# A fused tile kept in PSUM over four rotating banks, with every tail on VectorE

## The reference

```python
def ffn(x):                                   # x: (2, 512, 256)
    gate = silu((x @ q(gate_w)) * gate_scale) # (.., 768)
    up = (x @ q(up_w)) * up_scale
    return ((gate * up) @ q(down_w)) * down_scale

x = x + attention(layernorm(x))
x = x + ffn(layernorm(x))
x = x + s4d(layernorm(x))
x = x + ffn(layernorm(x))
```

## Time and profile before

| | before |
|---|---|
| median of three runs | 141.35 us (141.25 to 142.14) |
| span of the profiled execution | 140.5 us |
| mean granted clock of TensorE | 0.942 |
| TensorE matmul busy | 118.3 us (84%), 650 instructions |
| VectorE busy | 105.1 us (75%), 244 |
| GpSimd busy | 100.1 us (71%), 156 |
| ScalarE busy | 62.3 us (44%), 117 |
| tails on GpSimd (line 408) | 12, 14.6 us |
| tails on VectorE (line 850) | 12, 9.7 us |
| fuses on VectorE (line 843) | 24, 17.5 us |
| heads on ScalarE (line 560) | 24, 15.0 us |

### The profile page before, as it was taken

How to read it: one execution, slowest core, us unless ns; L and a number is a source line. 1 busy time by engine, 2 the same in 40 slices (tenths; PEclk the granted TensorE clock), 3 DMA queues, 4 the chain that set the end, 5 groups by cost and what they waited for, 6 DMA issues and landing times.

```text
span 140.5 us, 2050 instructions
## 1 busy us (share of the span) xinstructions
PE 118.3 (84%) x650; PEld 78.2 (56%) x650; DVE 105.1 (75%) x244; ACT 62.3 (44%) x117; POOL 100.1 (71%) x156
## 2 busy tenths in 40 slices
PE   5489999999999700899999999794999896999950
PEld 5466587585877400785456844453745465446640
DVE  0459999998885896059735699999999998656272
ACT  3124156532331103644795437394454474374500
POOL 6282899998899998997864175669879883029621
PEclk9968999999999995559999999999999999999996
DMA  3999700000000020000000000000000000001304
GB/s 129 281 320 361 225 3 7 2 0 0 0 1 0 0 71 4 7 0 0 0 0 0 0 0 0 2 0 0 0 0 0 0 0 5 0 0 40 109 0 149
DMA packets 5599, 6.03 MB, mean 43 GB/s; under 512 B 900, under 2 KB 4952, under 8 KB 5592
## 3 DMA queue, kind: packets, MB, share of 16 engines
q1 hardware_dynamic: 5464, 5.91, 12.8%
q0 software_dynamic: 128, 0.03, 0.1%
HBM read 4.89 MB, written 1.05 MB: 42 GB/s over the span
## 4 chain that ended last, share of the span: by engine, by line
PE 29%; DVE 29%; POOL 25%; issue 6%; ACT 4%; DMA 3%; SPq 1%; POOLq 0%; DVEq 0%; ACTq 0%
PE psum L1064 15%; PE psum L1077 7%; POOL s4d L304 5%; DVE stats L594 4%; PE psum L1002 3%; DMA x_in<-in_x 3%; DVE fused L843 3%; DVE scaled_down L791 3%; POOL rstd L280 3%; DVE h_rows L832 3%; PE psum L1025 2%; POOL gate L390 2%; POOL up L390 2%; POOL gate_raw L386 2%; POOL up_raw L386 2%
## 5 line engine op out<-in xcount | busy, mean ns | idle before, releaser
L408 POOL TENSOR_TENSOR f_tail<-fused,f_head 128x512 f16<-128x512 f32 x12 | 14.6, 1219 | 15.2 <-ACT f_head L560 15.2
L549 ACT ACTIVATE gated<-psum,scales 128x512 f32<-128x512 f32 x24 | 16.3, 681 | 15.0 <-PE psum L1064 15.0
L1077 PE MATMUL psum<-down,f_head 128*128 128x256 bf16 x96 | 22.0, 273 | 0.1
L1077 PE MATMUL psum<-down,f_tail 128*128 128x256 bf16 x96 | 22.0, 273 | 0.0
L843 DVE SCALAR_TENSOR_TENSOR fused<-psum,up_scales_fit,gated 128x512 f32<-128x512 f32 x24 | 17.5, 738 | 4.7 <-PE psum L1064 3.0
L560 ACT ACTIVATE f_head<-fused 128x512 f16<-128x512 f32 x24 | 15.0, 626 | 10.7 <-DVE fused L843 10.5
L1064 PE MATMUL psum<-h_head,up 128*128 128x512 f16 x48 | 14.3, 379 | 1.3 <-DVE fused L843 1.3
L850 DVE TENSOR_TENSOR f_tail<-fused,f_head 128x512 f16<-128x512 f32 x12 | 9.7, 809 | 7.1 <-ACT f_head L560 7.1
L1064 PE MATMUL psum<-h_tail,up 128*128 128x512 f16 x48 | 14.3, 379 | 0.0
L1064 PE MATMUL psum<-h_head,gate 128*128 128x512 f16 x48 | 14.3, 379 | 0.0
L1064 PE MATMUL psum<-h_tail,gate 128*128 128x512 f16 x48 | 14.3, 379 | 0.0
(11 more groups left out here) (168 smaller groups left out, 267.9 us busy)
## 6 DMA issues: line engine op xcount, KB each, us to landing
x_in<-in_x SPq DMA_DIRECT2D x4, 256.0 KB, 4.4
out<-x_in SPq DMA_DIRECT2D x4, 256.0 KB, 2.1
qkv_sb<-in_qkv SPq DMA_DIRECT2D x3, 256.0 KB, 3.9
gate_raw<-in_gate_w SPq DMA_DIRECT2D x1, 768.0 KB, 6.8
up_raw<-in_up_w SPq DMA_DIRECT2D x1, 768.0 KB, 8.6
down_raw<-in_down_w SPq DMA_DIRECT2D x1, 768.0 KB, 10.3
wo_sb<-in_o_proj SPq DMA_DIRECT2D x1, 256.0 KB, 5.1
taps_all<-taps_dram SPq DMA_DIRECT2D x1, 256.0 KB, 3.0
```

Source lines behind the costliest of these rows:

```text
L408: pool.tensor_tensor(f_tail[:, m, :], fused[:, m % FUSED, :], f_head[:, m, :], ALU.subtract).then_inc(f_tail_by_pool, 1)
L549: act.activation(gated[:, m % 2, :], psum[:, BANK_GATE[m % 2], :], ACT.Silu, scale=gate_scales[:, m:m + 1]).then_inc(gated_ready, 1)
L1077: last = pe.matmul(column(BANK_DOWN[t // 2], H * (t % 2), H), part[:, m, t * P:t * P + P], down16[:, m, :], start=(m == 0 and t % 2 == 0 a ...
```

## The change

- `fused` is no longer a tile in SBUF: `fuse` writes in place over up's PSUM bank, and head and tail read it there.
- Up has the banks 7, 3, 4, 5, 7, 3 for the tiles 0 to 5, so four banks go round; 4 and 5 are those of the transposed rows, which are free once `h_tail` is made.
- GpSimd makes no tails (all three of its tails in each pass are gone from its program). VectorE makes all six of a pass, one tile behind its fuse where the order is regular; in passes 1 and 2 the hand-written order is as in the diff, with fuse 5 moved behind `norm_rows`.
- TensorE's up matmuls wait for the tail that frees their bank, no longer for the fuse two tiles back. `turn_h` waits for the first four tails of the pass and no longer for `h_tail`.
- The loop over passes in TensorE's program is written out four times.

```diff
-        FUSED = 4
-        fused = sb("fused", [P, FUSED, S])
...
-        POOL_TAILS = (1, 3, 4)
-        DVE_TAILS = tuple(m for m in range(M) if m not in POOL_TAILS)
...
-        BANK_H, BANK_GATE, BANK_UP, BANK_DOWN = [4, 5], [6, 2], [7, 3], [0, 1]
+        BANK_H, BANK_GATE, BANK_UP, BANK_DOWN = [4, 5], [6, 2], [7, 3, 4, 5, 7, 3], [0, 1]
...
-                    act.activation(f_head[:, m, :], fused[:, m % FUSED, :], ACT.Copy).then_inc(f_head_ready, 1)
+                    act.activation(f_head[:, m, :], psum[:, BANK_UP[m], :], ACT.Copy).then_inc(f_head_ready, 1)
...
-                if i >= FUSED and (m - FUSED) % M in POOL_TAILS:
-
-                    dve.wait_ge(f_tail_by_pool, len(POOL_TAILS) * ((i - FUSED) // M) + POOL_TAILS.index((m - FUSED) % M) + 1)
-                dve.scalar_tensor_tensor(out=fused[:, m % FUSED, :], in0=psum[:, BANK_UP[m % 2], :],
+                dve.scalar_tensor_tensor(out=psum[:, BANK_UP[m], :], in0=psum[:, BANK_UP[m], :],
                                          scalar=up_scales_fit[:, m:m + 1], in1=gated[:, m % 2, :],
                                          op0=ALU.mult, op1=ALU.mult).then_inc(fused_ready, 1)
...
-                dve.tensor_tensor(f_tail[:, m, :], fused[:, m % FUSED, :], f_head[:, m, :],
-                                  ALU.subtract).then_inc(f_tail_by_dve, 1)
+                dve.tensor_tensor(f_tail[:, m, :], psum[:, BANK_UP[m], :], f_head[:, m, :],
+                                  ALU.subtract).then_inc(f_tail_ready, 1)
...
                     fuse(n, 2)
+                    tail(n, 1)
                     x3_stats(first)
                     s4d_begin(second)
                     fuse(n, 3)
+                    tail(n, 2)
                     s4d_end(second)
-                    tail(n, 2)
                     x3_stats(second)
                     fuse(n, 4)
-                    fuse(n, 5)
+                    tail(n, 3)
                     for k in second:
                         norm_rows(k)
+                    fuse(n, 5)
+                    tail(n, 4)
                     tail(n, 5)
                 else:
-                    for m in range(M):
+                    fuse(n, 0)
+                    for m in range(1, M):
                         fuse(n, m)
-                        if m in DVE_TAILS:
-                            tail(n, m)
+                        tail(n, m - 1)
+                    tail(n, M - 1)
...
-                    if m >= 2:
-                        pe.wait_ge(read, n * M + (m - 1))
+                    if w is gate16 and m >= 2:
+                        pe.wait_ge(gated_ready, n * M + (m - 1))
+                    if w is up16 and m >= 4:
+                        pe.wait_ge(f_tail_ready, n * M + (m - 3))
+                    if w is up16 and m < 2 and n >= 1:
+                        pe.wait_ge(f_tail_ready, (n - 1) * M + m + 5)
...
+                pe.wait_ge(f_tail_ready, n * M + m + 1)
+                if n == 0:
+                    pe.wait_ge(down_ready, m + 1)
...
-            with pe.Fori(0, 2 * B - 1) as n:
-                ffn_pass(n)
-                turn_h(n + 1, 0)
-                down(n, M - 3)
-                turn_h(n + 1, 1)
+            for n in range(2 * B):
+                for m in range(M):
+                    gate_up(n, m)
+                    if m >= LAG:
+                        down(n, m - LAG)
+                if n + 1 < 2 * B:
+                    pe.wait_ge(f_tail_ready, n * M + 4)
+                    turn_h(n + 1, 0, first=True)
+                    down(n, M - 3)
+                    turn_h(n + 1, 1, first=True)
+                else:
+                    down(n, M - 3)
                 down(n, M - 2)
                 down(n, M - 1)
```

More of the change, by code:

```diff
@@ L175, in hybrid_layer @@
         fused_ready, f_head_ready = sem("fused_ready"), sem("f_head_ready")
-        f_tail_by_pool, f_tail_by_dve = sem("f_tail_by_pool"), sem("f_tail_by_dve")
+        f_tail_ready = sem("f_tail_ready")
         down_made, down_read = sem("down_made"), sem("down_read")
@@ L403, in _ @@
                 inverse_std(1, k, 2, negative_mean=True)
[L405 to L409, removed]
             def residual(n, new, old, tiles, ready):
@@ L432, in _ @@
                     inverse_std(2, first, 2, negative_mean=(n == 1))
-                    if n == 1:
-                        tail(n, POOL_TAILS[0])
-                    else:
+                    if n == 2:
                         settle()
@@ L442, in _ @@
                         add_lag(3)
-                        tail(n, POOL_TAILS[0])
                     inverse_std(3, first, 2, negative_mean=True)
-                    tail(n, POOL_TAILS[1])
                     inverse_std(3, first + 2, 2)
-                    tail(n, POOL_TAILS[2])
                     if n == 1:
                         lag_tap()
[L450 to L455, removed]
+                if n == 3:
+                    residual(1, x4, x3, range(T), x4_by_pool)
             residual(1, x4, x3, (T, T + 2), x4_by_pool)
@@ L1056, in gate_up @@
             def gate_up(n, m):
-                for w, banks, made, read in ((gate16, BANK_GATE, gate_made, gated_ready), (up16, BANK_UP, up_made, fused_ready)):
-                    if m >= 2:
-                        pe.wait_ge(read, n * M + (m - 1))
+                for w, bank, made in ((gate16, BANK_GATE[m % 2], gate_made), (up16, BANK_UP[m], up_made)):
+                    if w is gate16 and m >= 2:
[4 more added lines that the diff above has]
+                        pe.wait_ge(f_tail_ready, (n - 1) * M + m + 5)
                     for part, ready in ((h_head, h_head_ready), (h_tail, h_tail_ready)):
@@ L1063, in gate_up @@
                                 pe.wait_ge(ready, n * C + (c + 1))
-                            last = pe.matmul(column(banks[m % 2], 0, S), w[:, c, m * P:m * P + P], part[:, c, :],
+                            last = pe.matmul(column(bank, 0, S), w[:, c, m * P:m * P + P], part[:, c, :],
                                              start=(part is h_head and c == 0), stop=(part is h_tail and c == C - 1))
@@ L1083, in _ @@
             LAG = 3
-            def ffn_pass(n):
+            for n in range(2 * B):
                 for m in range(M):
@@ L1090, in ffn_pass @@
                         down(n, m - LAG)
-            with pe.Fori(0, 2 * B - 1) as n:
-                ffn_pass(n)
-                turn_h(n + 1, 0)
-                down(n, M - 3)
-                turn_h(n + 1, 1)
+                if n + 1 < 2 * B:
[5 more added lines that the diff above has]
+                    down(n, M - 3)
                 down(n, M - 2)
                 down(n, M - 1)
-            ffn_pass(2 * B - 1)
-            for m in range(M - LAG, M):
-                down(2 * B - 1, m)
 _INS = ['x', 'qkv', 'o_proj', 'gamma', 'beta', 'd_param', 'log_dt', 'a_real_log', 'a_imag', 'c_re', 'c_im',
```

## The result

The changed kernel took 143.42 us, the median of 13 runs (141.71 to 144.05), against 141.59 for the kernel before in its own 13 (141.00 to 142.23). The ratio is 1.011, 95% interval 1.0085 to 1.0136: slower by about 1.6 us, or 1.1%, where 141.35, no change, was forecast. The ratio leaves out the three slowest runs of the kernel after (143.85 us and more, each over 1.5% above its fastest), and the medians of all 13 are 1.83 us apart. The time is above the stated range (up to 143.3) and above A's own range (up to 142.3).

A forecast was written before the change was run, and what follows sets the result against it. VectorE was taken to bound the two middle passes, TensorE the outer two. Terms of -0.11 (second pass) and +0.14 (third) summed to +0.03 on a 140.5 us span, plus 0.85 around it: 141.35 us, range 140.2 to 143.3.

The forecast's parts named there:

- A: Main forecast for the whole kernel: the trade of tails on VectorE comes out even, 140.8 to 142.3 us; chance 0.53.
- TensorE's waits: Feed-forward passes: dropped waits for fused give 0; added waits for tails 3, 4 and 5 also cost 0.
- The trade on VectorE: Middle passes: added tails and longer round trip against shorter stretched instructions; second pass -0.11 us, third +0.14.
- In-place writes: Twelve fuses on the path writing PSUM: taken as 0, keeping -0.4 to +0.4 us; far end +7 us.
- Rival C: Fuses on VectorE: PSUM writes are slow, by a second trip through the bank, up to 148 us; chance 0.05.
- Rival D: VectorE instructions with PSUM operands carry a fixed extra, 0.065 us for each of ten tails, 142.0 us; chance 0.08.
- Rival B: Middle passes: VectorE's stretched instructions do not shrink, as other GpSimd work moves under them; +2.5, 143.9 us; chance 0.16.
- Rival E: Middle passes: lag_tap does not hold norm_rows (-0.76 us) and the 107.68 pair goes to 0.87 (-0.48), 140.1 us; chance 0.18.
- What lies around the span: Outside the profiled span of 140.5 us: 0.85 us up to the median 141.35, carried along unchanged.

The follow-up runs named there:

- experiment 1: Changed kernel plus six useless 512-column matmuls on TensorE in the second and third pass, ahead of the wait for tail 3; ratio 0.994 to the kernel before.
- experiment 2: Changed kernel with gate and up of tile 5 moved behind down of tile 2 in the second and third pass; ratio 0.999 to the kernel before.
- experiment 8: Changed kernel with two filling matmuls (0.43 us) ahead of the wait for tail 3 in the second and third pass; ratio 0.999 to the kernel before.
- experiment 5: Changed kernel with six filling matmuls in the third pass alone, none in the second; ratio 0.999 to the kernel before.

## Why the prediction was wrong, point by point

**The step that failed** is the one on TensorE's waits: "Tail 3 ends just ahead of norm_rows, and the first-half transposes and the next down fit under norm_rows: 0." At full clock the term 0 holds, as experiments 1, 2 and 8 show, though in the third pass not for the reason given. In the second pass the two fit (the second half starts 0.05 us behind `norm_rows`). In the third, `norm_rows` takes 0.73 us and the two take 1.37, so that the second half starts 0.76 behind it (116.50 against 115.74, experiment 1); this costs nothing because VectorE has fuse 5 and the tails 4 and 5 to make until 117.77. I counted the added wait as time, on an engine with time to spare, and took the granted clock of 1.00 over from the earlier trace rows as if it were a property of the kernel. The idle time of 2.04 us in one piece brought the clock to 0.50, and at that pace the two do not fit: the second half of the transposes started 0.82 us after `norm_rows` in the second pass (97.33 against 96.51) and 1.82 in the third (118.21 against 116.39). In both passes VectorE's own work behind `norm_rows` lasts some 2.0 us. In the second that hid nearly all, and only 0.16 came through. In the third, VectorE stood idle for 1.10 us until `h_head` was there, `h_tails` came 1.44 later than with the clock kept (20.88 against 19.44), and the fourth pass started with TensorE behind, 0.36 more. The sum of both, 59.90 - 57.93 = 1.97 us, is the loss. No rival of mine had it: all five were about VectorE, GpSimd and PSUM.

**The trade on VectorE** was right. With the clock kept, the milestones are 57.92 to 57.94 against 57.82 before, +0.11, where the sum had +0.03. By pass: 19.78 to 19.80 (19.78 forecast), 19.43 to 19.45 (19.34), 18.70 (18.73). Norm_rows measured 1.54 and 0.74 against 1.50 and 0.74. The gap from its end to `h_tails` was 1.94 and 1.95 in experiment 1, for 1.97.

**In-place writes**: I took 0 and kept both ends.

```profile
L820 DVE SCALAR_TENSOR_TENSOR psum<-psum,up_scales_fit,gated x24: 725/754/760, 66.3 to 133.4; 128x512 f32<-128x512 f32 x24
```

The median fuse is 0.754 against 0.742; six times that 0.012 would be 0.07 of the 0.10 us that the third pass had above the sum. Rival C (a second trip through the bank) is out. Rival D is out as well: the tails with PSUM input have a median of 0.681.

```profile
L827 DVE TENSOR_TENSOR f_tail<-psum,f_head x24: 675/681/692, 67.7 to 134.8; 128x512 f16<-128x512 f32 x24
```

Here, too, the trace does not show the 62 cycles that the Trainium skill (VectorE: DVE Perf Modes, "The TRN2 errata") puts between the two sources.

**Rival B** (the stretched instructions do not shrink) is refuted by the 0.87 and 0.74 above; the 1.54 of `norm_rows` in the second pass is what the sum itself had (1.50). **Rival E** is refuted in its first half: `x_lag` does hold `norm_rows`, 1.54. The `s4d_end` pair of the third pass kept its 1.35.

**What lies around the span**: I took 0.85 us, the median less the span. In the runs since, each with its own span, it is 1.8 (143.69 against 141.9). For the kernel before it is 2.0 (142.28 against 140.3). By an estimate from that, the profiled execution before took about 142.5, more than the median, and it was slower ahead of the passes. That did not touch the sum, since both went out of the same execution.

**What stays open**: why 2.04 us brought the fall in two of three gaps that were profiled, and about 2.7 us in one of two; and why experiment 1 ran 0.6% below the kernel before. Every idle stretch of up to 1.92 us that is named here left the clock alone. That the fall costs what was lost is shown by experiments 1, 2 and 8, where the transposes wait for the same tail and only the clock behind it differs, and by the second pass of 5, where the full gap without a fall cost nothing. A full gap without a fall was not seen in the third pass.

## What to carry to other kernels

A wait added to an engine with slack is not free when it gathers that slack into one piece: on TensorE look how long the longest idle stretch becomes and what must run right behind it, and treat the granted clock as something that a change can move. If independent work stands on either side of such a wait, move it into the gap; here that cost nothing and undid the whole loss. And compare two profiles by milestones of the same work rather than by the span, so that the noise ahead of the stage drops out.

## What the runs showed of the hardware that was not expected

- TensorE's clock fell from its upper to its lower level after 2.04 us without work, twice in one execution, and came back some 3.9 us after work began (95.09 to 99.00); the same gap in an execution of experiment 5 left it at 1.00.
- A VectorE instruction that reads and writes the same PSUM bank in place takes 12 ns more than one that reads PSUM and writes SBUF (754 against 742 for 128x512), and ScalarE's head takes 593 ns from PSUM against 626 from SBUF.
- Two `norm_rows` instructions take 1.54 us beside GpSimd's products and 0.74 without them, about one product of 0.7 us more.
